# Graph layer over 16 batches: sums turned once for two batches, next batch's h turned behind the sums, last two products in halves

## The reference

```python
h = jnp.maximum(_layernorm(x, axis=-1), 0.0)              # x: 16 x 512 x 128
# A1 = A2 = adj (16 x 512 x 512), seven relations r:
A_list = [adj, adj, shifted, adj^T, adj^T, shifted^T, eye]
HW  = einsum('bnf,rfo->rbno', h, W[:, :F]) + einsum('rd,rdo->ro', W_edges, W[:, F:])[:, None, None, :]
AHW = einsum('rbnm,rbmo->rbno', A, HW)
x   = x + max(AHW, axis=0) + b
```

## Time and profile before

| | |
|---|---|
| median of 3 runs | 205.43 us (205.3 to 205.56) |
| the profiled execution, its own time | 205.48 us |
| its span, first to last instruction | 203.7 us |
| granted TensorE clock, mean | 0.999 |
| busy: PE, DVE, ACT, POOL | 97%, 83%, 79%, 57% |
| period of one batch in the middle | 11.8 us |

### The profile page before, as it was taken

How to read it: one execution, slowest core, us unless ns; L and a number is a source line. 1 busy time by engine, 2 the same in 40 slices (tenths; PEclk the granted TensorE clock), 3 DMA queues, 4 the chain that set the end, 5 groups by cost and what they waited for, 6 DMA issues and landing times.

```text
span 203.7 us, 3448 instructions
## 1 busy us (share of the span) xinstructions
PE 197.7 (97%) x918; PEld 151.2 (74%) x918; DVE 170.0 (83%) x411; ACT 160.1 (79%) x432; POOL 115.8 (57%) x162
## 2 busy tenths in 40 slices
PE   6999999999999999999999999999999999999991
PEld 6456466778787787878778787878878787887871
DVE  3487969989898998989989898998989899878565
ACT  3887989996969879696988969697896969795230
POOL 4041341477574938657592956759295675939500
PEclk9999999999999999999999999999999999999999
DMA  5999999997888979789987969799795969570501
GB/s 161 333 356 358 373 346 273 293 357 191 258 315 232 350 183 342 201 269 306 292 304 162 381 153 333 228 246 357 198 395 107 312 199 343 208 154 0 100 4 51
DMA packets 33748, 51.07 MB, mean 251 GB/s; under 512 B 1873, under 2 KB 11329, under 8 KB 33729
## 3 DMA queue, kind: packets, MB, share of 16 engines
q1 hardware_dynamic: 31152, 46.53, 67.1%
q0 software_dynamic: 2304, 4.20, 13.3%
q10 hardware_dynamic: 272, 0.13, 0.2%
HBM read 46.65 MB, written 4.19 MB: 250 GB/s over the span
## 4 chain that ended last, share of the span: by engine, by line
PE 94%; DMA 2%; DVE 2%; SPq 0%; issue 0%; DVEq 0%
PE bank_p L870 13%; PE bank_p L871 11%; PE bank_p L872 10%; PE bank_g L832 6%; PE bank_g L835 6%; PE bank_g L841 6%; PE bank_gT L818 6%; PE bank_gT L812 6%; PE bank_gT L808 6%; PE bank_p L741 3%; PE bank_p L860 3%; PE bank_p L749 3%; DMA adj_sb<-in_adj_dram 2%; PE bank_g L789 2%; PE bank_gT L780 2%; PE bank_g L770 2%
## 5 line engine op out<-in xcount | busy, mean ns | idle before, releaser
L334 POOL TENSOR_TENSOR a_lo<-adj_sb,a_hi 128x512 fp32r<-128x512 f32 x26 | 33.1, 1296 | 31.6 <-DVE a_lo L596 28.5
L640 DVE TENSOR_TENSOR best<-bank_p,best 128x512 f32<-128x512 f32 x48 | 33.1, 691 | 7.2 <-PE bank_p L872 6.0
L422 ACT ACTIVATE a_hi<-adj_sb 128x512 fp32r<-128x512 f32 x56 | 34.5, 620 | 1.3 <-DMA adj_sb<-in_adj_dram 1.3
L431 ACT ACTIVATE aT_hi<-adjT_sb 128x512 fp32r<-128x512 f32 x56 | 34.4, 620 | 0.0
L341 POOL TENSOR_TENSOR aT_lo<-adjT_sb,aT_hi 128x512 fp32r<-128x512 f32 x26 | 33.2, 1297 | 0.9 <-ACT aT_hi L431 0.3
L327 POOL TENSOR_TENSOR o_sb<-best,x_bias 128x512 f32<-128x512 f32 x15 | 19.8, 1317 | 19.1 <-DVE aT_lo L603 15.9
L637 DVE SCALAR_TENSOR_TENSOR best<-bank_p,c_col,best 128x512 f32<-128x512 f32 x32 | 24.0, 750 | 6.6 <-ACT best L480 6.0
L461 ACT ACTIVATE gT_hi<-bank_gT 128x512 fp32r<-128x512 f32 x16 | 9.5, 595 | 25.0 <-PE bank_gT L818 24.7
L443 ACT ACTIVATE h<-x_sb,shift,rstd 128x128 f32<-128x128 f32 x60 | 24.7, 488 | 0.0
L870 PE MATMUL bank_p<-hT_hi,w_hi 128*128 128x512 f32 x48 | 20.0, 417 | 0.0
L872 PE MATMUL bank_p<-hT_lo,w_hi 128*128 128x512 f32 x48 | 18.7, 390 | 0.0
(11 more groups left out here) (122 smaller groups left out, 477.7 us busy)
## 6 DMA issues: line engine op xcount, KB each, us to landing
adj_sb<-in_adj_dram SPq DMA_DIRECT2D x15, 1024.0 KB, 7.5
adjT_sb<-in_adjT_dram SPq DMA_DIRECT2D x15, 1024.0 KB, 8.3
x_bias<-in_biasT_dram SPq DMA_DIRECT2D x16, 256.0 KB, 6.5
x_bias<-in_xT_dram POOLq DMA_DIRECT2D x16, 256.0 KB, 4.1
x_sb<-in_x_dram SPq DMA_DIRECT2D x15, 256.0 KB, 8.3
out_dram<-o_sb SPq DMA_DIRECT2D x15, 256.0 KB, 5.5
adj_sb<-in_adj_dram SPq DMA_DIRECT2D x4, 256.0 KB, 5.1
adjT_sb<-in_adjT_dram SPq DMA_DIRECT2D x4, 256.0 KB, 5.1
```

What stands on the lines that cost most here:

```text
L334: nc.gpsimd.tensor_tensor(a_lo[q][:, c, :], adj_sb[q][:, c, :], a_hi[q][:, c, :].bitcast(F32), ALU.subtract).then_inc(alo_last_ready, 1)
L422: nc.scalar.activation(a_hi[q][:, c, :], adj_sb[q][:, c, :], ACT.Copy, accum_out=sums[q][:, 0, c:c + 1]).then_inc(ahi_ready, 1)
L431: nc.scalar.activation(aT_hi[q][:, c, :], adjT_sb[q][:, c, :], ACT.Copy, accum_out=sums[q][:, 1, c:c + 1]).then_inc(aThi_ready, 1)
L640: op = nc.vector.tensor_tensor(best[q][:, :], product, best[q][:, :], ALU.max)
```

## The change

Four things change.

**The sums are turned in pairs.** From batch 4 (`PAIRED`) on, an even batch leads and the odd one behind it follows. `sum_parts` has room for eight groups, of which a batch used four; the follower's sums now fill the other half, one `turn_sums` in the leader serves both, and one `copy_sumsT`. So batches 5, 7, ..., 15 have neither. For this the leader needs the follower's sums early: ACT makes both `split_adj(b+1)` and `split_adjT(b+1)` at the leader's beginning, ahead of `split_gT(b)`, POOL moves `part_sums(b+1)` up, and `turn_sums` waits for it. In the leader the high part of h goes behind `copy_sumsT` (`split_h`), and its low part on DVE behind that of g. `c_rows` has a second form for the followers.

**The next batch's h is turned earlier.** From batch 2 (`AHEAD`) on `turn_h(b+1)` stands behind `begin_products(b)`, in front of product 3, and writes `bank_gT`, which is free once gT(b) is split. ACT's `split_hT(b+1)` comes behind `begin_best(b)` (in a leader) or behind the first chunk of `split_adjT(b+1)` (else), DVE's low part between its second and third maximum.

**Loads.** adj(b+2) and adj^T(b+2) stand together in SP's list and from batch 5 on no longer wait for gT(b) and g(b), only for the splitting of the buffer that they fill.

**The last batch.** Products 5 and 6 are both made in halves, in the order 5 and 6 of the first half, then 5 and 6 of the second; the first half's x and bias are added by POOL.

```diff
+        def leads(b):
+            return b >= PAIRED and (b - PAIRED) % 2 == 0 and b + 1 < B
+        def follows(b):
+            return b >= 1 and leads(b - 1)
@@ SP
+                    if b - 2 <= FIRST:
+                        sp.wait_ge(gT_psum, b - 1)
...
                     load_adj(b + 2)
+                    load_adjT(b + 2)
                 store(b - 1)
@@ POOL, part_sums and the loop
+                q, turn, first = b % 2, turn_of(b), 4 * int(follows(b))
...
                 finish(b - 1)
+                if leads(b):
+                    part_sums(b + 1)
@@ ACT
                     split_adj(b + 1)
+                if leads(b):
+                    split_adjT(b + 1)
                 split_gT(b)
-                split_hT(b)
+                if b < AHEAD:
+                    split_hT(b)
...
                     make_h(b + 1)
+                    if not leads(b):
+                        split_h(b + 1)
                 split_g(b)
-                copy_sumsT(b)
+                if not follows(b):
+                    copy_sumsT(b)
+                if leads(b):
+                    split_h(b + 1)
                 begin_best(b)
...
+                elif leads(b):
+                    split_hT(b + 1)
+                elif b + 1 < B:
+                    split_adjT(b + 1, range(1))
+                    split_hT(b + 1)
+                    split_adjT(b + 1, range(1, C))
@@ DVE
+                for i in range(1, NPROD - NLAST * int(b == B - 1)):
+                    if i == NH and b + 1 < B:
+                        split_hT_lo(b + 1)
                     take_best(b, i)
@@ PE
+                if not follows(b):
+                    turn_sums(b)
                 for i in range(NH):
                     product(b, i)
                 begin_products(b)
+                if AHEAD <= b + 1 < B:
+                    turn_h(b + 1)
+                for i in range(NH, NPROD - NLAST * int(b == B - 1)):
                     product(b, i)
+            for i in range(2):
+                for k in range(NLAST):
+                    product(B - 1, NPROD - NLAST + k, HALVES[i], last_banks[k][i])
```

More of the change, by code:

```diff
@@ L20 @@
 NBEST = NPROD - 1
+NLAST = 2
 NH = len(H_RELS)
@@ L303, in part_sums @@
                     pool.wait_ge(aThi_ready, (b - FIRST + 1) * NS)
-                if b >= 2:
-                    pool.wait_ge(sumsT_psum, b - 1)
+                if turn >= 2:
+                    pool.wait_ge(sumsT_psum, turn - 1)
+                parts = sum_parts[turn % 2]
                 for copy in range(2):
-                    last = nc.gpsimd.tensor_copy(sum_parts[q][:, :, :, :, 2 * copy], s)
+                    last = nc.gpsimd.tensor_copy(parts[:, :, :, :, first + 2 * copy], s)
                 last.then_inc(parts_hi, 1)
@@ L310, in part_sums @@
                 for copy in range(2):
-                    last = nc.gpsimd.tensor_tensor(sum_parts[q][:, :, :, :, 2 * copy + 1], s,
-                                                   sum_parts[q][:, :, :, :, 2 * copy].bitcast(F32), ALU.subtract)
+                    last = nc.gpsimd.tensor_tensor(parts[:, :, :, :, first + 2 * copy + 1], s,
+                                                   parts[:, :, :, :, first + 2 * copy].bitcast(F32), ALU.subtract)
                 last.then_inc(parts_lo, 1)
@@ L385, in _ @@
                     split_adjT_last(b + 1)
-                    part_sums(b + 1)
+                    if not leads(b):
+                        part_sums(b + 1)
                     add_bias(b + 1)
+            b, q = B - 1, (B - 1) % 2
+            pool.wait_ge(xb_in[q], turns(b))
+            pool.wait_ge(stored[q], turns(b - 2))
+            pool.wait_ge(half_best_done, 1)
+            nc.gpsimd.tensor_tensor(o_sb[q][:, HALVES[0]], best[q][:, HALVES[0]], x_bias[q][:, HALVES[0]],
+                                    ALU.add).then_inc(half_out_ready, 1)
         @block.scalar
@@ L413, in sum_adjT, with split_adj @@
                 last.then_inc(sums_ready, 1)
-            def split_adj(b):
+            def split_adj(b, chunks=range(C)):
                 q = b % 2
@@ L420, in split_adj, with split_adjT @@
                 act.wait_ge(parts_lo, b - 1)
-                for c in range(C):
+                for c in chunks:
                     nc.scalar.activation(a_hi[q][:, c, :], adj_sb[q][:, c, :], ACT.Copy,
                                          accum_out=sums[q][:, 0, c:c + 1]).then_inc(ahi_ready, 1)
-            def split_adjT(b):
+            def split_adjT(b, chunks=range(C)):
                 q = b % 2
@@ L454, in split_hT @@
                     act.wait_ge(prod_psum, (b - 1) * NPROD + NH)
-                nc.scalar.activation(hT_hi[:, :], bank_h[:, 0:N], ACT.Copy).then_inc(hThi_ready, 1)
+                nc.scalar.activation(hT_hi[:, :], bank_h(b)[:, 0:N], ACT.Copy).then_inc(hThi_ready, 1)
             def split_gT(b):
@@ L613, in split_hT_lo @@
                 dve.wait_ge(hThi_ready, b + 1)
-                nc.vector.tensor_tensor(hT_lo[:, :], bank_h[:, 0:N], hT_hi[:, :].bitcast(F32),
+                nc.vector.tensor_tensor(hT_lo[:, :], bank_h(b)[:, 0:N], hT_hi[:, :].bitcast(F32),
                                         ALU.subtract).then_inc(hTlo_ready, 1)
@@ L645, in _ @@
             groups = ident[:, :].rearrange("p (g s) -> p g s", s=GROUP)
-            nc.vector.tensor_reduce(row_hi[:, :], groups[:, :, 0:2], AXIS.XY, ALU.add)
-            nc.vector.tensor_reduce(row_lo[:, :], groups[:, :, 2:4], AXIS.XY, ALU.add).then_inc(masks_ready, 1)
+            for s in range(2):
+                nc.vector.tensor_reduce(row_hi[:, s:s + 1], groups[:, :, 4 * s:4 * s + 2], AXIS.XY, ALU.add)
+                last = nc.vector.tensor_reduce(row_lo[:, s:s + 1], groups[:, :, 4 * s + 2:4 * s + 4], AXIS.XY, ALU.add)
+            last.then_inc(masks_ready, 1)
             first_variance(0, half_stats_done, half_aggr_done)
@@ L716, in _ @@
                     split_adj_lo(b + 1)
+                    if not leads(b):
+                        split_h_lo(b + 1)
+                split_g_lo(b)
+                if leads(b):
                     split_h_lo(b + 1)
-                split_g_lo(b)
-                for i in range(1, NPROD - int(b == B - 1)):
+                for i in range(1, NPROD - NLAST * int(b == B - 1)):
+                    if i == NH and b + 1 < B:
+                        split_hT_lo(b + 1)
                     take_best(b, i)
@@ L922, in _ @@
                     aggregate_T(b)
-                turn_h(b)
+                if b < AHEAD:
+                    turn_h(b)
                 if b < FIRST:
@@ L927, in _ @@
                     aggregate(b)
-                turn_sums(b)
+                if not follows(b):
+                    turn_sums(b)
                 for i in range(NH):
@@ L931, in _ @@
                 begin_products(b)
-                for i in range(NH, NPROD - int(b == B - 1)):
+                if AHEAD <= b + 1 < B:
+                    turn_h(b + 1)
+                for i in range(NH, NPROD - NLAST * int(b == B - 1)):
                     product(b, i)
-            for nodes, to in zip(HALVES, last_banks):
-                product(B - 1, NPROD - 1, nodes, to)
+            for i in range(2):
+                for k in range(NLAST):
+                    product(B - 1, NPROD - NLAST + k, HALVES[i], last_banks[k][i])
 def kernel(x, adj, L0_gnn_W, L0_gnn_W_edges, L0_gnn_b):
```

110 lines of the change are left out of this document (66 added, 44 removed).

## The result

| | before | after |
|---|---|---|
| median of the runs, us | 205.5 (205.3 to 206.31, 4 runs) | 210.1 (209.97 to 211.82, 4 runs) |
| profiled execution, us | 205.48 | 209.97 |
| its span, us | 203.7 | 208.2 |
| batch in the middle | 11.80 | leader 12.58, follower 11.57 |

The ratio is 1.0234, with a 95% interval of 1.0196 to 1.0271: 2.3% slower. The prediction was 206.6 us with a range to 208.6, and 0.6 for slower. So the side was right and the size was not: 1.2 us were forecast and 4.6 measured, outside the range.

The account below looks back on a forecast made before the run. PE, at 11.80 us per batch set by its matmul count, was taken as the bound. Pairs +1.31, batch 2 +0.15 and the end -0.26 gave +1.2 us on 205.43: 206.6 us, range 203.3 to 208.6.

Parts of the forecast that it names:

- DVE and ACT have 1.2 and 1.6 us of slack: Per batch: DVE busy 10.64 and ACT 10.21 of 11.81 us; shortening PE's list gains until one is late.
- ACT's leg, 11.31 us: From the turn of a leader's h to the end of its sums' copy: 11.31 us on ACT, without any wait.
- PE's wait of 0.71 per leader: PE stands 0.71 us before product 2 in each leader; less 0.46 saved, +0.25 us per pair.
- The rival that it is shorter than summed: ACT's leg in leaders is shorter than summed; 202.5 us with no wait; chance 0.3 for over 0.4 us faster.
- The two are one wait, not two: In leaders, part of PE's wait stands before the turned sums, for POOL's splitting, within the same 0.71 us.
- The turn of h at its full price: On PE, the moved turn of h still costs 0.47 us; 0.12 less per batch was kept for the range.
- The end, -0.26: DVE's chain in the last batch gets 0.26 us shorter; bounds 0 and -0.5.
- Batch 2, 0.15: ACT's wait before hT_hi delays batch 2's splitting; the sums' copy comes late for product 2, costing 0.15 us.
- I cost it at nothing; if that cover is gone it costs 0 to 0.5 per follower.: In followers DVE is some 0.3 us ahead of PE at begin_products; costed at nothing, otherwise 0 to 0.5 each.
- The second rival: Much slower: follower's adj^T late, 207.5 to 212 us, or DVE late in followers, 209.6; chance 0.12 together.
- no square root to take, which gives back 0.19: In the last leader ACT has no square root, giving back 0.19 us: pairs total +1.31 instead of +1.50.
- adj^T's load late in followers: Follower's adj^T lands past the 9.5 us from issue to need; 6 us per microsecond late; costed at nothing.

Follow-up runs that it names:

- run 5: Changed kernel with POOL splitting the follower's sums ahead of its addition of the previous batch's bias in leaders; 210.3 us, ratio 1.0234.
- run 6: Kernel of run 5 with ACT also splitting all four chunks of adj^T ahead of hT_hi of a leader; 205.31 us, ratio 0.9991.
- run 1: Changed kernel without pairs (PAIRED = 16), keeping the moved turn of h, the loads and the halves; 205.34 us, ratio 0.9993.
- run 3: Kernel before the change with only the last two products in halves and POOL's half addition; 205.52 us, ratio 0.9992.
- run 9: Changed kernel with the store and the bias's load ahead of adj^T's load again for the first batches; 211.38 us, ratio 1.0297.
- run 8: Changed kernel with h turned and split in its old places, and POOL splitting the sums before its bias addition in leaders; 203.58 us, ratio 0.9914.
- run 10: Kernel of run 8 with the store and the bias's load ahead of adj^T's load for the first batches; 203.14 us, ratio 0.9891.
- run 7: Changed kernel with POOL's bias addition in two halves outside leaders, the second behind DVE's h_lo; 208.61 us, ratio 1.0154.
- run 4: Changed kernel with four unused bn_stats and four bn_aggr added on DVE in batch 14; 209.03 us, ratio 1.0166.

## Why the prediction was right or wrong

- **PE is the engine whose list sets the batch, and DVE and ACT have 1.2 and 1.6 us of slack.** Right, and right too that order and not shares decides: PE's work fell and the time rose.
- **ACT's leg, 11.31 us, and PE's wait of 0.71 per leader.** Right: 11.21, a wait of 0.71, and a leader of 12.58 for 12.5. Runs 5 and 6 show that this leg by itself makes leaders long. The rival that it is shorter than summed, with 0.3 the heaviest of the others, is out: its 202.5 us did not come, since the relief of PE made ACT and POOL late. The rule of improving the most-contended engine was read too simply beside it. The same section, Identifying Performance Opportunities in the Trainium skill's "Perfetto Trace Analysis", judges TensorE's headroom not by the busy share of its matmuls but, among others, by that of its weight loads; that is 74% in the earlier trace rows, under DVE's 83%. So the miss of the 202.5 does not speak against the rule.
- **"The two are one wait, not two" (POOL's splitting of the sums).** Right in its size but for a reason half seen. I had POOL's split begin when ACT was done with adj^T; it begins when the bias's addition is done, which waits for DVE. So these are two legs by different ways, each of about the whole length, and that the forecast of the leader came out with only one of them summed is luck: with POOL's list first, run 5, the leader stays as long.
- **The turn of h at its full price, 0.12 kept back for the range.** It measured 0.41 for 0.47 (and the batch in run 1 is 0.08 shorter): between the two.
- **The end, -0.26.** DVE's chain gave 0.20, the execution 0.07 to 0.1 (run 3): within the bounds, at the dear end.
- **Batch 2, 0.15.** The mechanism was right and its size low: ACT's late copy holds product 2 for 0.33. The other half of the 0.66 was not seen: POOL's addition, late behind a late bias, meets `shift`, 0.32 in front of the four matmuls of the sums. An early bias gave back 0.31 (run 9), and in the kernel with h in its old place, where ACT is not late, all of it (runs 8 and 10). The total up to batch 4 came out (0.70 for 0.62) since other terms were smaller than forecast.
- **Followers: "I cost it at nothing; if that cover is gone it costs 0 to 0.5 per follower."** This is the first step that failed. It measured 0.23 as a gap, 0.31 by run 7, 1.5 us in all. I had summed DVE's list from the durations of before and found 0.3 us to spare. But hT_lo was not only 0.6 us of DVE's list: it was what kept POOL's addition from `shift`. A duration of before was taken over into a place where it has another neighbour. The second rival had this case (DVE late in the followers, up to 3 us), under a 0.12 that it shared with the load; its time of 209.6 was near the measured one, for half its reason.
- **The last leader: "no square root to take, which gives back 0.19".** The second step that failed: it lost 1.48 more than the forecast instead. I looked at what ACT is spared there and not at what DVE is spared, and DVE's missing statistics let it run into POOL. That cost 1.2 us by run 4, and the 0.19 did not come back there either.
- **adj^T's load late in followers.** It did not happen: ACT's leg has no wait for it.

With the two steps undone, 210.1 less 1.5 (run 7) and 1.1 (run 4) is 207.5, an estimate, since the two edits were not run together.

What stays open: when a gap of PE is followed by a fallen clock, and whether ACT's leg alone, with POOL's order left, would cure the leader.

## What to carry to other kernels

Two moves that cost nothing alone can cost 2% together: price the leg through every engine that the pair of them makes, from the place where the earlier move now lets it start. When an instruction is moved off an engine, ask what it was standing beside, and not only how long it took: in these runs a VectorE operation with one input in PSUM was a good neighbour for a GpSimd operation that reads SBUF (0.68 to 0.69 us with it and without), and one with two SBUF inputs was not. And look at the first and the last turn of a loop by their own lists, for every engine; missing work there shifts who meets whom.

## What the runs showed of the hardware that was not expected

- A VectorE operation of four columns took 0.69 to 1.27 us instead of 0.16 beside a GpSimd addition, and it ended with it. GpSimd's 16-column casts took 1.28 and 1.22 instead of 0.34 and 0.44 beside VectorE's SBUF-to-SBUF splits. Where both were long (run 6, at 111.0), DVE's two splits took 2.37 instead of 1.28 and POOL's addition 1.80 instead of 1.29, so that both together, 111.00 to 113.37, took little less than one behind the other. VectorE's operations with one PSUM input and `bn_stats` kept their times.
- Adding 1.2 us of work to VectorE made the kernel 1.07 us faster (run 4).
- After gaps of 1.64 and 1.77 us TensorE's granted clock was 0.64 and 0.62 in the following 4 us, and run 9's last leader took 15.26; in the changed kernel and in run 7 a gap of 1.78 was not followed by that in the profiled execution (their last leaders took 13.77 and 13.78).
